# Two cross-attention and mixture-of-experts blocks: maxima transposed in one fp32r pass, query groups 1 to 3 prepared between units

## What is computed

```
x = x + xattn0(LN(x), ctx)   # 16 heads of 8; inside: LN again, rotary positions, bias, gate
x = x + ffn0(LN(x))          # 2 of 8 experts for each token, 128 -> 512 -> 128, silu
x = x + xattn1(LN(x), ctx)   # 16 heads of 8, plain
x = x + ffn1(LN(x))          # 2 of 8 experts, at most 321 rows an expert
```

## Time and profile before

| | us |
|---|---|
| three runs, median | 325.83 |
| lowest and highest | 324.19, 326.91 |
| the profiled execution, span of its instructions | 324.3 |
| TensorE busy in it | 250.7 |
| VectorE, ScalarE, GpSimd busy | 155.1, 118.2, 137.8 |

### The profile page before, as it was taken

The page is one execution under the profiler, slowest core; times in us unless marked ns, Lnnn a source line. Parts: engine busy times, 40 slices in busy tenths (PEclk is TensorE's granted clock), DMA queues, the critical chain, the costliest instruction groups (busy, mean ns, idle before and its releaser), DMA issues.

```text
span 324.3 us, 5466 instructions
## 1 busy us (share of the span) xinstructions
PE 250.7 (77%) x2044; PEld 197.2 (61%) x2044; DVE 155.1 (48%) x497; ACT 118.2 (36%) x206; POOL 137.8 (42%) x178
## 2 busy tenths in 40 slices
PE   2767999999975539999942989989987338999800
PEld 2645766667754427999941775545555328999800
DVE  3878425363775364242211964276878303332205
ACT  4033637755321023443500067965540204423200
POOL 5744602630156441355562400641267631456640
PEclk9999999999975558999995799999999959999975
DMA  7999970200011017000013920200010125001015
GB/s 241 269 224 377 219 161 2 65 3 2 0 36 34 33 33 197 16 20 26 23 36 127 361 116 0 66 1 2 0 37 33 33 82 141 15 31 36 26 29 181
DMA packets 26819, 27.02 MB, mean 83 GB/s; under 512 B 3193, under 2 KB 23844, under 8 KB 26534
## 3 DMA queue, kind: packets, MB, share of 16 engines
q1 hardware_dynamic: 23797, 21.58, 24.6%
q0 software_dynamic: 2560, 4.08, 3.9%
q10 hardware_dynamic: 432, 0.98, 0.9%
HBM read 16.76 MB, written 10.79 MB: 85 GB/s over the span
## 4 chain that ended last, share of the span: by engine, by line
PE 49%; issue 20%; DVE 13%; DMA 6%; POOL 5%; ACT 3%; another core or an unknown queue 1%; SPq 1%; POOLq 0%; DVEq 0%; ACTq 0%
PE ps L1201 8%; PE ps L1406 6%; PE ps L1178 6%; PE ps L1395 5%; PE ps L1162 4%; PE ps L1153 4%; PE ps L1133 3%; PE ps L1184 2%; DMA xres<-x 2%; DMA xe<-back 2%; DVE cst L813 2%; DMA sent<-hidk,slotu 1%; DVE attT L814 1%; PE ps L1217 1%
## 5 line engine op out<-in xcount | busy, mean ns | idle before, releaser
L559 POOL DMA_INDIRECT back<-probT,pairu x48 | 46.5, 970 | 37.4 <-DVE probT L992 15.1
L1133 PE MATMUL ps<-blank,ident 128*128 128x256 f32 x90 | 28.6, 479 | 23.6 <-DMA sent<-hidk,slotu 13.0
L1406 PE MATMUL ps<-w,hT 128*128 128x128 f32 (+1 forms) x384 | 45.0, 274 | 0.0
L804 DVE TENSOR_REDUCE peak<-ps 128x8 f32<-128x616 f32 x32 | 25.5, 798 | 40.2 <-PE ps L1153 40.2
L1406 PEld LDWEIGHTS ps<-w,hT 128*128 128x128 f32 (+1 forms) x384 | 44.2, 183 | 0.0
L654 ACT ACTIVATE probT<-ps 77x1024 f32<-77x1024 f32 x32 | 32.7, 1022 | 27.7 <-PE ps L1184 15.5
L518 POOL DMA_INDIRECT sent<-hidk,slotu x32 | 31.9, 997 | 16.4 <-issue 9.8
L1133 PEld LDWEIGHTS ps<-blank,ident 128*128 128x128 f32 x90 | 21.1, 244 | 28.5 <-issue 14.0
L531 POOL TENSOR_TENSOR w1lo<-hT,w1hi 128x1024 fp32r<-128x1024 f32 x8 | 18.9, 2366 | 40.0 <-ACT w1hi L628 40.0
L1178 PE MATMUL ps<-qst,kst 100*78 100x256 f32 x128 | 29.1, 300 | 1.0 <-ACT qst L638 1.0
L500 POOL TENSOR_SCALAR vare<-mv 128x2 f32<-128x2 f32 (+2 forms) x17 | 3.8, 226 | 52.8 <-DVE mv L786 52.3
(11 more groups left out here) (158 smaller groups left out, 474.1 us busy)
## 6 DMA issues: line engine op xcount, KB each, us to landing
sent<-blank SPq DMA_DIRECT2D x16, 193.5 KB, 8.5
xe<-sent SPq DMA_DIRECT2D x16, 193.5 KB, 4.0
back<-blank SPq DMA_DIRECT2D x16, 128.0 KB, 4.8
hT<-w1b SPq DMA_DIRECT2D x4, 512.0 KB, 6.0
w<-w2b SPq DMA_DIRECT2D x1, 2048.0 KB, 13.5
xe<-back SPq DMA_DIRECT2D x8, 256.0 KB, 3.5
hT<-w1d SPq DMA_DIRECT2D x4, 512.0 KB, 5.5
w<-w2d SPq DMA_DIRECT2D x1, 2048.0 KB, 11.4
```

The lines of the kernel that those rows point to most:

```text
L559: pool.indirect_dma_start(back[m], bass.IndirectOffsetOnAxis(ap=pairu[0:n, e, c:c + 1], axis=0), ye[0:n, e, c, :], None, bounds_check=NPAI ...
L804: dve.tensor_reduce(peak[:, u % 2], s, AX.X, ALU.max, negate=True).then_inc(s_peak[a], 1)
L1133: pe.matmul(ps[:, bank, 0:GQ], ident[:], blank[:, 0:2, 0:D], start=True, stop=True)
L1406: last = pe.matmul(ps[0:n, 6 + e % 2, c * P:(c + 1) * P], hT[:, e % 2, f, c * P:c * P + n], w2[:, e, f, :], start=(f == 0), stop=(f == FC ...
```

## The change

Six things change.

1. `maxima`: the peaks and the identity become fp32r (`identr`, read elsewhere as fp32 through `ident`), and the result goes to a bank of its own, 5 (`BMX`), instead of rows 96 to 99 of the shifted scores' banks.
2. Numerator and denominator share bank 4 (`BND`); only the first matmul of a group clears it.
3. Queries of all groups pass through banks 6 and 7 (`BY`, and `BR` for tokens and the stack's second half). Only group 0 is prepared ahead of the units; groups 1, 2 and 3 have their steps between the units, in both blocks. Rotary sum and low part move from GpSimd to VectorE, the bias parts from VectorE to GpSimd.
4. The two norms at the start of block 1 become one scale of x, (v (1 + eps) + eps^2)^-0.5 (`twice_normed`), without statistics of `hid`; `hid` itself is made later, between units.
5. The later steps stand one unit later for groups 0 to 2 and as before for the last group; `due` yields the last group's steps behind the others. The weight casts move from turns 6 to 9 and 3 to 6 to turns 9 to 12.
6. Warm-ups fall from 13 to 6 and from 12 to 6. `numden`, `rden` and `yT` lie in `hid` instead of `cst`.

```diff
-WARM_START = 13
-WARM_SUM = 12
+WARM_START = 6
+WARM_SUM = 6
...
-DVE_STEPS = [dict(attended=5, projected3=6, residual3=7, hidden3=9, projected=8, residual=9, hidden=10,
-                  choose=12, slots=13, next_context=11, next_parts=13, next_keys=14, choose3=11, slots3=12),
-             dict(attended=5, residual=7, hidden=8, choose=10, slots=11)]
...
+DVE_STEPS = [dict(attended=5, projected3=6, residual3=7, hidden3=9, projected=9, residual=10, hidden=11,
+                  choose=13, slots=14, next_context=11, next_parts=13, next_keys=14, choose3=11, slots3=12),
+             dict(attended=5, residual3=7, hidden3=8, choose3=10, slots3=11, residual=8, hidden=9, choose=11, slots=12)]
...
+PE_QUERIES = [[(-1, "tokens", 0), (-1, "queries", 0), (-1, "tokens", 1), (-1, "keys", 0), (-1, "stack", 0),
+               (0, "queries", 1), (1, "tokens", 2), (3, "stack", 1), (4, "queries", 2), (4, "tokens", 3),
+               (6, "stack", 2), (7, "queries", 3), (9, "stack", 3)],
...
+WEIGHT_TURNS = [[9, 10, 11, 12], [9, 10, 11, 12]]
...
-        peak = sb("peak", [P, 2, GT, Q4])
+        peak = sb("peak", [P, 2, GT, Q4], F32R)
...
+            def twice_normed(b):
+
+                s = of_batch(b)
+                count[0] += 1
+                pool.wait_ge(s_var, count[0])
+                link(pool.tensor_scalar(vtwice[:, s], mv[:, s, 1], 1.0 + EPS, EPS * EPS, ALU.mult, ALU.add))
+                pool.tensor_tensor(rtwice[:, s], vtwice[:, s], power[:, s], ALU.pow).then_inc(s_rstd, 1)
...
             def maxima(a, u):
...
-                    last = pe.matmul(ps[ST:ST + Q4, BK + u % 2, i * P:(i + 1) * P], peak[:, u % 2, i, :], ident[:],
-                                     start=True, stop=True)
+                    at = GQ * (u % 2) + i * P
+                    last = pe.matmul(ps[0:Q4, BMX, at:at + P], peak[:, u % 2, i, :], identr[:], start=True, stop=True)
...
-                for bank in (BNUM, BDEN):
+                for den in range(2):
                     for q in range(Q4):
...
+                        w = onepad[:, j, :] if den else vpad[:, b, Q4 * q + j, :]
+                        last = pe.matmul(ps[32 * q:32 * q + 32, BND, den * GQ:den * GQ + GQ], w,
+                                         probT[0:KV, u % RING, q, :], start=(j == 0 and not den), stop=(j == UG - 1),
+                                         skip_group_check=True)
...
             def stack_q(a, g):
 
                 pe.wait_ge(s_qlo, GROUPS * a + g + 1)
-                if a == 0 and g == 1:
-                    pe.wait_ge(s_kvfree, 1)
+                if g >= 1:
+                    pe.wait_ge(s_qstD, GROUPS * a + g)
+                    pe.wait_ge(s_inT, min(g + 2, GROUPS) if a == 0 else GROUPS + g + 1)
```

More of the change, by code:

```diff
@@ new lines @@
+ACT_STEPS = [dict(projected3=4, tanh3=5, projected=6, tanh=8, copies3=8, turned3=9, copies=9, turned=10),
+             dict(copies3=9, turned3=7, copies=10, turned=8)]
+POOL_STEPS = [dict(deviation=11, residual=13, send=16),
+              dict(deviation=6, residual=8, send=11)]
+PE_QUERIES = [[(-1, "tokens", 0), (-1, "queries", 0), (-1, "tokens", 1), (-1, "keys", 0), (-1, "stack", 0),
+               (0, "queries", 1), (1, "tokens", 2), (3, "stack", 1), (4, "queries", 2), (4, "tokens", 3),
+               (6, "stack", 2), (7, "queries", 3), (9, "stack", 3)],
+              [(-1, "tokens", 0), (-1, "queries", 0), (-1, "stack", 0), (0, "tokens", 1), (1, "queries", 1),
+               (3, "stack", 1), (4, "tokens", 2), (5, "queries", 2), (6, "stack", 2), (7, "tokens", 3),
+               (8, "queries", 3), (9, "stack", 3)]]
@@ new lines @@
+DVE_QUERIES = [[(-1, "rotated", 0), (-1, "values", 0), (-1, "low", 0), (-1, "keys", 0), (-1, "stack", 0),
+                (0, "norm", 1), (0, "rotated", 1), (1, "hidden", 0), (2, "low", 1), (3, "stack", 1),
+                (4, "rotated", 2), (4, "hidden", 1), (5, "low", 2), (5, "keys", 1), (6, "stack", 2),
+                (7, "rotated", 3), (8, "low", 3), (9, "stack", 3)],
+               [(-1, "sum", 0), (-1, "sum", 1), (-1, "norm", 0), (-1, "norm", 1), (-1, "low", 0), (-1, "stack", 0),
+                (0, "sum", 2), (1, "norm", 2), (2, "low", 1), (3, "stack", 1), (3, "sum", 3), (4, "norm", 3),
+                (5, "low", 2), (6, "stack", 2), (8, "low", 3), (9, "stack", 3)]]
@@ L1325, in project_q @@
                 pe.wait_ge(s_inT, GROUPS * a + g + 1)
[L1326 to L1329 removed]
+                if g >= 1:
+                    pe.wait_ge(s_qstA, GROUPS * a + g)
+                last = pe.matmul(ps[:, BY, 0:GQ], weight(f"q{a}"), q, start=True, stop=True)
                 if a == 0:
[L1331 removed]
+                    last = pe.matmul(ps[:, BY, GQ:2 * GQ], weight("q0p"), q, start=True, stop=True)
                 last.then_inc(s_q, 1)
```

257 lines of the change are left out of this document (124 added, 133 removed).

## The result

The changed kernel takes 344.83 us (median of 4 runs, 341.27 to 347.67) where the kernel before takes 326.37 beside it: 1.053 times as long, 95% interval 1.044 to 1.063. I had forecast 320.7 and a range up to 327.5. The change makes the kernel slower by 5%, and the prediction was wrong in sign and in size. Some executions of one and the same kernel are slower than the rest at a lower granted clock; every ratio given with an interval is of the fast ones alone, so it can differ from the quotient of the medians, and the profiled execution of after, at 347.67, is the slowest of its four.

A forecast was written before the change was run, and what follows sets the result against it. The prediction took TensorE to bound the units, by only 0.45 us; -8.6 - 1.9 + 4.6 - 2.8 + 1.1 + 2.5 = -5.1 took the span from 324.3 to 319.2, 320.7 as the runs' median, range 314.5 to 327.5.

The forecast's parts named there:

- Rival (d): Block 2's queries or block 1's sparse start run longer at clock 0.50, about 3 us doubles: 323.5; chance 11%.
- +0.5: Body of block 1: ScalarE's weight casts of 1.05 now fall in shorter units, costing 0.5 us.
- +1.5: Block 2: turn(0) waits for hidden(0), behind attended(1), whose product collides with GpSimd's weight split: 1.5 us.
- body of block 2: Block 2's units: shorter maxima against added query work, division, casts and a collision, +1.1 us with the last exp.
- Start of block 1: Up to exp 3 of block 1: less VectorE preparation brings exp 3 from 42.65 to about 34.0, -8.6 us.
- Body of block 1: Behind exp 3: 12 units save 0.40 each, query work and casts moved there cost some back, -1.9 us.
- rival (c): The fp32r maxima transposes save only half, or the exp loop takes the gain: 325; chance 13%.
- Tail of block 1: Behind block 1's units: gate(2) waits for a later projected(2), so project(3) starts 8.9 behind the last unit, +4.6 us.
- Rival (b): Block 1's tail doesn't stretch, because ScalarE and VectorE reach numerator 3 early: 316; chance 18%.
- Start and body of block 2: Shorter warm-up and earlier queries leave -2.8 us at the fifth unit; the body with the last exp adds +1.1.
- Tail of block 2: Behind block 2's units: hidden(2) behind attended(3) and turn(2) ahead of project(3), with transposes, copy and logits, +2.5 us.
- Rival (a): Late low parts at six hand-offs stop the units; gain gone from 0.85 each, 331 at 1.7 each; chance 13%.

The follow-up runs named there:

- g1: After with weight splits at turns 4, 7, 8, 9 (block 1) and 3 to 6 (block 2), two unread matmuls ahead of each turn(0): 326.83 us, 0.997 of before.
- e2: After with the warm-ups put back to 13 and 12: 351.23 us, 1.055 of before.
- e7: After with unread matmuls ahead of turn(0), 4 in block 1 and 9 in block 2: 330.47 us, 1.010 of before.
- f3: After with splits at turns 7, 8, 10, 11 and 3 to 6, unread matmuls ahead of turn(0), maxima in fp32: 341.82 us, 1.047 (1.009 with fp32r).
- g3: g1 with the later-step tables of before in both blocks: 319.12 us, 0.974 of before.
- g2: g1 with the later-step tables of before in block 2 only: 323.88 us beside 326.58, 0.992 by the medians, no interval.
- e3: After with both the old weight turns (6 to 9, 3 to 6) and the old warm-ups (13, 12) put back: 339.66 us, 1.010 of before.
- h1: g3 without the unread matmuls ahead of turn(0): 318.89 us, 0.959 of before (0.926 to 0.992).
- b3: Before with unread matmuls behind its units: block 1's tail, the waits for scattered rows, block 2's gather: 329.79 us, 1.013 of before.

## Why the prediction was wrong, step by step

**The failed step is the clock.** The sum took every unit at full rate. Rival (d) had the clock, at 11%, in the wrong place and at the wrong price: "Six query stages of TensorE, about 3 us, double: 323.5". It looked at the preparation of the queries. There the half rate did come (19.9 to 33.6, and 194.0 to 204.2 of block 2). In after's trace it goes with an exp 3 at 37.9, 3.9 behind the forecast and 4.5 behind g1, which has the same warm-ups and full rate there; so this part of the rival was a hit, in this execution. e2 shows that the longer warm-up is no cure: it takes what the clock gives. The larger loss was elsewhere: filling the two stops is worth 14 us (e7), most of it half rate within the units that TensorE bounds, which set in at stops of 1.6 and 4.2. The rows of before that I read at 0.50 lie ahead of the units, and the sum never asked what a stop within them would do to the rate.

**The step under it is the weight turns.** I had the move of `WEIGHT_TURNS` to 9 to 12 as "+0.5" in block 1 and as "+1.5" for the one collision in block 2. The direction was right, and the wait too: `turn(0)` for `hidden(0)`, beside a split. The instruction was another: I had the product of `attended(1)` collide, and in after's trace none of the eight products does (L831, 0.42 to 0.43 each); `hidden(0)` itself does. The sizes were not right: 4.60 in block 2, since its two instructions each stood beside a split, and in block 1 the deviation queued behind the split, a wait that I hadn't listed, as GpSimd's queue wasn't followed past the split. I had the collision's longest case, 2041 ns, and priced the stop by itself, not what follows from it. (The terms listed for the body of block 2 also add up to +1.35, not +1.1, which changes nothing here.)

The Trainium skill (SBUF — State Buffer, "SBUF: two separate sides") lets the one that starts first hold the shared pair for its whole instruction: a GpSimd operation that reads SBUF, or a VectorE operation with two SBUF inputs or in a two-port mode. By that rule every such VectorE step that meets a running split waits for its end. The traces agree: 2.43 beside 2.34 for the low part, 2.25 beside 2.37 for the product, 4.60 beside 4.65 for the two instructions of the norm, one split each (which of the conditions the norm meets no trace shows). In the prediction I drew on the page for the start of block 1 alone, where the sum took 1.11 instead of 0.4 (16.03 in after's timeline), a small matter.

**Start of block 1: right.** Forecast 19.9, 24.1 and 34.0 for first scores, exp 0 and exp 3. In after 20.5, 26.2 and 37.9, with half rate from 19.9 to 33.6; in g1, with the clock up, 19.4, 23.3 and 33.4.

**Body of block 1: right but for the clock.** Forecast -1.9 from exp 3 to exp 15; after +1.9, g1 -3.5. A pair of fp32r maxima takes 71.40 - 71.28 = 0.12, forecast 0.13, and rival (c) falls: in f3 fp32 costs 0.5 a unit, where I had 0.40.

**Tail of block 1: the mechanism right, and the size where the clock is up.** Forecast +4.6, with a hole of 2 to 3 us ended by VectorE's L840, and `project(3)` 8.9 behind the last unit. In after the last unit ends at 92.94 + 1.08 = 94.0:

```profile
98.26 0.76 PE L1254 MATMUL ps<-row,one 1*128 1x128 f32 x2 [2.14 <-DVE hidb L840]
...
101.75 1.19 PE L1242 MATMUL ps<-attT,sqw 128*128 128x256 f32 x2 [0.40 <-ACT norm L678]
```

That is a hole of 2.14 and 7.8. The stage is +4.9 in g1 and +9.0 in after, whose last units lie wholly in the half rate. With the old tables it is +1.2 in g3's trace, so the later steps make 3.7 of it. Rival (b) falls.

**Start and body of block 2: right.** Forecast -2.8 and, with the last exp, +1.1. The stage to the first scores is -3.1 in g1 and -3.4 in after; from there to exp 15 it is 0 in g1, +7.6 in after.

**Tail of block 2: mis-sized.** Forecast +2.5, measured +6.4 in g1 and +7.5 in after. g2 shows that it is the later step table, as I had said, worth 6.1 and not 2.5. I counted three steps of group 3's own chain; that the rest is group 2's whole chain (norm, transposes, choice, slots), which stands a unit later ahead of it, I take from the tables, and no run separates it.

**Rival (a), that hand-offs stop the units,** was half a hit: its time (331) was nearer than mine, for a reason that wasn't there in after, whose two long stops are at `turn(0)`. The waits at L1340 that it named are there where a low part is blocked (2.59 in e3), but its price of 0.85 a hand-off assumed that the wait itself is the cost.

Taken together: the forecast's span was 319.2. g1's profiled execution, which has the change without the collisions, has 319.8, the shortest of its ten runs, and by its ratio g1 stands at 325.4; so the rest of the sum is off by some 5, of which the tail of block 2 is 3.9. After loses the other 18 or so to splits and clock. With the step tables put back as well, the change is worth 2.6% (g3, interval 1.8 to 3.4); h1's time is the same.

## What to carry to other kernels

Where one engine is the bound and its clock can fall at a stop, the stop costs twice: its own length, and the half rate of what follows. Look for stops in the stretches that this engine bounds; in the tail of small dependent steps holding the rate with fills won nothing in before (b3). When work is moved between VectorE and GpSimd, write down for each long GpSimd operation which VectorE steps with SBUF operands fall beside it in the new order, and who waits for them. A table that was tuned for one order can be wrong for the next, in its old form and shifted: here both the old turns of block 1 (6 to 9) and the new (9 to 12) collided, at different steps, and turns 4, 7, 8 and 9, chosen from a trace of the new order, did not.
